# Second copies of the high halves in the first attention's stack: from GpSimd to ScalarE, under an order of its own

## The chip, the cores and the metric

The kernel runs on one core of one Trainium2 chip. The metric is device time in microseconds (us) of one execution. A core has five engines that run side by side, each working through its own queue in order: TensorE (PE in the rows; PEld is its weight load), VectorE (DVE), ScalarE (ACT), GpSimd (POOL) and SyncE (SP, which issues most of the DMA). They wait for one another only through semaphores.

## What is computed

A post-norm transformer block on 16 sequences of 256 rows of 128 features: attention with four key heads shared by sixteen query heads, a layer norm, then a second block (pre-norm attention and a mixture of experts, where each row goes to the one expert with the highest gate), and a last layer norm. The part that the change touches is the first attention's queries and keys:

```
q = (x @ w_q).reshape(B, S, 16, 8);  k = (x @ w_k).reshape(B, S, 4, 8)
q = _apply_rope(_rms_norm(q), cos, sin);  k = _apply_rope(_rms_norm(k), cos, sin)
scores = einsum('bqhd,bkhd->bhqk', q, repeat(k)) / sqrt(8)
scores = tanh(scores / 50) * 50      # then causal mask, softmax, @ v, @ w_o
x = layernorm(x + attention);  x = layernorm(x + block2(x))
```

## The kernel before

One sequence of 256 rows is a batch; there are 16 (`n` = 0 to 15), and each lies on 128 partitions as two tiles. Every batch goes through stages named by letters: **a** loads x, projects, rotates and normalises q and k and splits them; **b** computes scores, tanh, exp and mask in six units; **c** multiplies by v, projects and normalises; **d**, **e**, **f** are the second attention and the gate, with eight units in d and e; **g** is the expert part, in 40 tiles of 128 rows, some of it as early as batch 12.

A step, such as `a_stack` of batch 5, is a short function on one engine. The table `ORDER` gives each step of each batch a rank; every engine issues its own steps in the order of their ranks. So the table, written out by hand as numbers, sets all queues. Each engine's queue is in order: a step that waits holds everything behind it on that engine.

The scores' matmuls take float16, so q and k are each split into a high half and a remainder. `a_sum` (VectorE, L1085 to L1093) makes the mean squares; `a_pow` (GpSimd, L1411) takes them to the power -1/2 (for batches 0 and 1 `a_root` does this on VectorE); `a_split` (VectorE) multiplies (L1121, `qn`), casts the high half into columns 0 to 7 of each head's 32 columns of `stack1` (L1126, step name `hi`), and puts the remainder into columns 24 to 31 (L1128, step name `lo`). `a_stack` (GpSimd, helper `move` at L1414) then makes four copies so that one product of 32 columns gives all cross terms. Queries are 128x256 elements, keys 128x64. After it `a_qT` (TensorE, L725, eight transposes) and `a_kT` (L733) turn the stack, VectorE copies the result (`qs`, L1134, and `kT`, L1139), and the scores' matmuls of `b_sc` (L749) start. `d_stack` uses the same helper line L1414 for the second attention: two copies per batch.

Around these, in the same queues: on ScalarE `b_tanh` (L973), `b_exp` (L977), `e_exp` (L1004), and copies out of PSUM such as `a_xTc` (L968), `c_sum` (L982), `f_sum` (L1009), `f_oTc` (L1013), `d_xTc` (L992); on GpSimd `b_mask` (L1430), `c_pow` (L1435), `c_x1` (L1445, L1449), `f_scatter` (L1478); on VectorE `d_max` (L1230).

PSUM is used in turns. `ring_s` has two buffers, used alternately by the units of `b_sc`, `d_mx` and `e_sc` in the order of their ranks; `ring_p` has two for most other products. Before a unit writes, TensorE waits (`claim`) until the reader of the unit two turns back is done: for `b_sc4` that reader is `b_tanh4`.

`w_fill` (L701, or L698 in the shape of four column groups) is a matmul of a blank tile into the buffer that is free next. It computes nothing; 428 of them stand between other TensorE steps.

Of the kernel before, what the change touches and what calls it, by code (L numbers as in the profile page):

```python
# [106 lines left out]
def wait_turn(eng, sem, n, buffers, each):  # L107
# [16 lines left out]
    "a_load": (0, 3, 5, 6, 15, 246, 410, 500, 593, 824, 927, 1050, 1226, 1468, 1509, 1684),  # L124
    "a_xTc": (1, 13, 19, 113, 189, 293, 424, 584, 703, 864, 1002, 1187, 1346, 1511, 1634, 1815),
    "a_xT": (2, 7, 17, 70, 165, 257, 392, 534, 693, 865, 987, 1153, 1292, 1497, 1620, 1785),
    "a_qkv": (4, 12, 64, 128, 224, 377, 506, 652, 822, 984, 1093, 1265, 1422, 1593, 1776, 1898),
    "a_rope": (8, 18, 69, 134, 234, 387, 511, 657, 820, 986, 1114, 1270, 1440, 1607, 1791, 1920),
    "a_sum": (9, 20, 81, 139, 245, 389, 513, 665, 842, 1003, 1143, 1272, 1477, 1617, 1805, 1924),
# [1391 lines left out]
```

## Time and profile before

| | |
|---|---|
| median of three runs | 705.04 us (702.55 to 707.58) |
| the profiled execution | 702.71 us, its span 701.0 us |
| mean granted TensorE clock, share of full | 0.927 |
| PE busy | 570.1 us, 81% |
| DVE busy | 480.9 us, 69% |
| ACT busy | 425.4 us, 61% |
| POOL busy | 416.7 us, 59% |

The span runs from the first to the last instruction; 1.7 us of the profiled execution's own time lie outside it. In rows of groups, the first part says which line, engine and operation, `out<-in` and how many; behind the first bar are the busy time and the mean of one; behind the second the engine's idle time before them and what ended it. In rows of a timeline the first number is the start, the second the duration in us.

### The profile page before, as it was taken

How to read it: one execution, taken by the hardware profiler on the slowest of the kernel's cores; microseconds unless marked ns; L12 is line 12 of the kernel's file. 1: busy time of each engine (PE TensorE's matmuls, PEld its weight loads, DVE VectorE, ACT ScalarE, POOL GpSimd, SP SyncE). 2: the span in 40 equal slices, each digit the busy share in tenths (PEclk: the TensorE clock that was granted, in tenths of full speed). 3: DMA queues.
4: the chain of work that ended last, by engine and by line, in shares of the span. 5: the costliest groups of instructions: out<-in, count | busy, mean ns of one | idle time of the engine just before them, and what ended most of it. 6: DMA issues, size and time to landing. Idle time of an engine off the chain costs nothing.

```text
span 701.0 us, 16358 instructions
## 1 busy us (share of the span) xinstructions
PE 570.1 (81%) x5771; PEld 339.1 (48%) x5771; DVE 480.9 (69%) x1356; ACT 425.4 (61%) x650; POOL 416.7 (59%) x443
## 2 busy tenths in 40 slices
PE   2648888888888878888897898878997899888992
PEld 1324333344445444455454554545553555557992
DVE  3546757868678868587867768687777787635452
ACT  1675376676785666757677596756675654534661
POOL 2469573648486953775757585769544235525664
PEclk9969779899999988799999999899998999999996
DMA  6420000000000100000012301001002022186650
GB/s 146 135 69 2 8 1 9 2 24 1 9 2 25 40 2 6 5 16 10 17 41 62 85 9 36 1 20 60 25 29 62 12 69 91 39 257 183 187 149 6
DMA packets 30143, 34.30 MB, mean 49 GB/s; under 512 B 6970, under 2 KB 21984, under 8 KB 30064
## 3 DMA queue, kind: packets, MB, share of 16 engines
q1 hardware_dynamic: 26096, 25.53, 12.9%
q0 software_dynamic: 2816, 6.43, 2.6%
q10 hardware_dynamic: 1152, 1.30, 0.6%
q8 instruction: 47, 0.77, 0.5%
q14 instruction: 32, 0.26, 0.1%
HBM read 22.37 MB, written 11.27 MB: 48 GB/s over the span
## 4 chain that ended last, share of the span: by engine, by line
PE 40%; DVE 23%; POOL 16%; issue 10%; ACT 7%; SPq 2%; DMA 1%; POOLq 0%; ACTq 0%; DVEq 0%
DVE mx L1230 10%; PE out L877 6%; POOL rs L1411 5%; PE ring_s L863 3%; POOL stack L1414 3%; PE out L762 3%; PE ring_p L943 3%; PE ring_p L701 3%; PE ring_s L843 3%; POOL p L1430 2%; ACT p L1004 2%; PE ring_p L814 2%; ACT p L973 2%; PE ring_s L749 2%; PE ring_p L931 1%
## 5 line engine op out<-in xcount | busy, mean ns | idle before, releaser
L1230 DVE TENSOR_REDUCE mx<-ring_s 128x4 f32<-128x1024 f32 x128 | 152.8, 1218 | 26.9 <-PE ring_s L843 26.1
L1004 ACT ACTIVATE p<-ring_s 128x1024 f32<-128x1024 f32 x128 | 126.3, 1027 | 38.8 <-PE ring_s L863 38.3
L973 ACT ACTIVATE p<-ring_s 128x1024 f32<-128x1024 f32 x96 | 97.1, 1022 | 38.5 <-PE ring_s L749 38.1
L1411 POOL TENSOR_TENSOR rs<-ms,small 128x40 f32<-128x40 f32 x14 | 94.8, 6772 | 27.6 <-DVE ms L1093 27.3
L1414 POOL TENSOR_SCALAR stack<-stack 128x256 f16<-128x256 f16 (+1 forms) x96 | 65.0, 700 | 75.7 <-DVE stack L1222 42.8
L1430 POOL TENSOR_SCALAR_AFFINE_SELECT p<-p 128x512 f32<-128x512 f32 (+1 forms) x96 | 75.8, 798 | 56.4 <-ACT p L977 56.3
L977 ACT ACTIVATE p<-p 128x1024 f32<-128x1024 f32 x96 | 100.2, 1057 | 0.7
L701 PE MATMUL ring_p<-blank 128*128 128x256 f16 x362 | 80.6, 286 | 5.1 <-ACT t_midT L1037 1.9
L877 PE MATMUL out<-p,v 128*32 128x256 f32 x1024 | 69.8, 400 | 1.3 <-DVE rb L1288 1.2
L843 PE MATMUL ring_s<-kc,qs 32*128 32x256 f16 x512 | 51.2, 281 | 20.2 <-DVE mx L1230 13.0
L863 PE MATMUL ring_s<-qs,kc 32*128 32x256 f16 x512 | 49.4, 290 | 10.1 <-DMA qs<-mT 4.5
L1489 POOL DMA_INDIRECT out<-t_y,t_idx x40 | 41.3, 1034 | 16.4 <-DVE t_y L1380 9.0
L701 PEld LDWEIGHTS ring_p<-blank 128*128 128x128 f16 x362 | 32.6, 103 | 37.9 <-issue 25.3
L762 PE MATMUL out<-p,v 128*32 128x256 f32 x512 | 47.0, 443 | 4.5 <-POOL p L1430 4.1
L749 PE MATMUL ring_s<-qs,kT 32*128 32x512 f16 x192 | 40.0, 422 | 9.7 <-DVE mx L1230 4.5
L1484 POOL TENSOR_TENSOR t_rs<-t_ve,small 128x1 f32<-128x1 f32 x40 | 23.5, 591 | 35.8 <-DVE t_idx L1375 35.5
L943 PE MATMUL ring_p<-w_down,t_midT 128*128 x320 | 44.0, 283 | 0.0
L1478 POOL DMA_INDIRECT routed_rows<-row,pos x32 | 32.9, 1027 | 15.4 <-issue 8.1
L877 PEld LDWEIGHTS out<-p,v 128*32 128x32 f32 x1024 | 29.1, 112 | 26.1 <-issue 11.9
L943 PEld LDWEIGHTS ring_p<-w_down,t_midT 128*128 128x128 f32 x320 | 40.5, 199 | 0.0
L843 PEld LDWEIGHTS ring_s<-kc,qs 32*128 32x128 f16 x512 | 15.3, 94 | 51.7 <-DVE mx L1230 26.4
L1037 ACT ACTIVATE t_midT<-ring_p,b_up 128x128 f32<-128x128 f32 x92 | 26.3, 368 | 21.7 <-PE ring_p L931 20.1
(162 smaller groups left out, 1111.5 us busy)
## 6 DMA issues: line engine op xcount, KB each, us to landing
w_up<-in_L_ffn_w SPq DMA_DIRECT2D x40, 256.0 KB, 2.8
t_row<-routed_rows SPq DMA_DIRECT2D x40, 132.0 KB, 2.4
routed_rows<-padrow SPq DMA_DIRECT2D x8, 396.0 KB, 3.2
...
qs<-mT SPq DMA_DIRECT2D x64, 2.0 KB
out<-t_y,t_idx POOLq DMA_INDIRECT x40, 2.4
...
```

The source lines that it names most:

```text
L701: nc.tensor.matmul(spare[:, 0:256], blank[:, 0:P], blank[:, 0:256], start=True, stop=True)
L843: mm = nc.tensor.matmul(bank(f"d_mx{j}", n)[:, z * 512 + g * S:z * 512 + (g + 1) * S], qs2[32 * i:32 * i + 32, n % 2, 2 * k + g, t * P:(t ...
L863: mm = nc.tensor.matmul(bank(f"e_sc{u}", n)[:, j * 512 + v * S:j * 512 + (v + 1) * S], kc2[32 * i:32 * i + 32, n % 2, g, keys * P:(keys + ...
L877: mm = nc.tensor.matmul(out2[32 * c:32 * c + 32, half * S:(half + 1) * S], v2[:, n % 2, keys, 8 * half + 2 * c + v, :], p2[:, u, at:at + S ...
L943: mm = nc.tensor.matmul(bank("g_down", s)[:, 0:D], t_midT[:, s % 2, c * P:(c + 1) * P], w_down[:, bass.ds(e * FF + c * P, D)], start=False ...
L973: nc.scalar.activation(p1[:, u], bank(f"b_sc{u}", n)[:], ACT.Tanh, scale=float(ISQ / CAP)).then_inc(b_s.sem, 1)
L977: nc.scalar.activation(p1[:, u], p1[:, u], ACT.Exp, scale=CAP).then_inc(b_x.sem, 1)
L1004: nc.scalar.activation(p2[:, u], bank(f"e_sc{u}", n)[:], ACT.Exp, scale=float(ISQ)).then_inc(e_s.sem, 1)
L1230: nc.vector.tensor_reduce(mx2[:, t, 2 * pair:2 * pair + 2, 2 * k:2 * k + 2], bank(f"d_mx{j}", n)[:].rearrange("p (z g s) -> p z g s", z=2, ...
L1411: nc.gpsimd.tensor_tensor(rs1[:], ms1[:], half, ALU.pow).then_inc(a_p.sem, 1)
L1414: return nc.gpsimd.tensor_scalar(dst, src, 1.0, None, ALU.mult)
L1430: nc.gpsimd.affine_select(out=w, in_=w, compare_op=ALU.is_ge, fill=0.0, base=0, pattern=[[0, w.shape[1]], [1, P]], channel_multiplier=-1). ...
```

## The change

Two of the four copies of `a_stack` move to a new ScalarE step `a_hi`: those that copy the high half (queries to columns 8 to 15, keys to columns 16 to 23). They need only `hi`, which VectorE finishes one instruction before `lo`. GpSimd keeps the two copies of the remainder. `a_qT` waits for both.

```diff
+        a_h = steps("a_h", "copy")
...
             def a_qT(n):
                 pe.wait_ge(a_p.sem, a_p.upto(n, "stack"))
+                pe.wait_ge(a_h.sem, a_h.upto(n, "copy"))
...
+            def a_hi(n):
+                act.wait_ge(a_v.sem, a_v.upto(n, "hi"))
+                s4 = stack1[:].rearrange("p (t h) e -> p t h e", t=T)
+                nc.scalar.copy(s4[:, :, 0:NH, HD:2 * HD], s4[:, :, 0:NH, 0:HD])
+                nc.scalar.copy(s4[:, :, NH:, 2 * HD:3 * HD], s4[:, :, NH:, 0:HD]).then_inc(a_h.sem, 1)
...
             def a_stack(n):
                 pool.wait_ge(a_v.sem, a_v.upto(n, "lo"))
                 s4 = stack1[:].rearrange("p (t h) e -> p t h e", t=T)
-                move(s4[:, :, 0:NH, HD:2 * HD], s4[:, :, 0:NH, 0:HD])
                 move(s4[:, :, 0:NH, 2 * HD:3 * HD], s4[:, :, 0:NH, 3 * HD:])
-                move(s4[:, :, NH:, HD:2 * HD], s4[:, :, NH:, 3 * HD:])
-                move(s4[:, :, NH:, 2 * HD:3 * HD], s4[:, :, NH:, 0:HD]).then_inc(a_p.sem, 1)
+                move(s4[:, :, NH:, HD:2 * HD], s4[:, :, NH:, 3 * HD:]).then_inc(a_p.sem, 1)
```

The whole table `ORDER` is new as well, a line of it before and after:

```diff
-    "a_stack": (14, 39, 111, 187, 283, 433, 555, 714, 908, 1045, 1195, 1365, 1552, 1677, 1851, 1982),
+    "a_hi": (18, 41, 118, 205, 284, 436, 590, 748, 899, 1092, 1232, 1393, 1555, 1692, 1846, 2002),
+    "a_stack": (23, 34, 133, 193, 287, 428, 593, 759, 928, 1083, 1213, 1389, 1546, 1709, 1849, 1993),
```

It keeps the plan in the large (which batches overlap which) and swaps neighbours in every queue; it has 447 `w_fill` instead of 428. Line numbers of the changed kernel are 3 to 10 higher.

ScalarE's queue around the split of batch 8, before. L977 is `b_exp` 2 and 3, L973 `b_tanh` 3 and 4 of batch 7, L1009 `f_sum` of batch 4, L1013 `f_oTc`.

```order
L977 ACTIVATE p<-p 128x1024
L973 ACTIVATE p<-ring_s 128x1024 x2
L1009 COPY sums<-out 128x512
L977 ACTIVATE p<-p 128x1024
L1013 COPY oT<-out 128x256
```

The same place after, where L983 is `b_tanh`, L1019 `f_sum`, L977 and L978 the new `a_hi` of batch 8, L972 `a_xTc`, L1023 `f_oTc`.

```order
L1019 COPY sums<-out 128x512
L983 ACTIVATE p<-ring_s 128x1024
L977 COPY stack<-stack 128x2x16x8
L978 COPY stack<-stack 128x2x4x8
L983 ACTIVATE p<-ring_s 128x1024
L972 COPY xT<-ring_p 128x256
L983 ACTIVATE p<-ring_s 128x1024
L1023 COPY oT<-out 128x256
```

`a_hi` of batch 8 now stands between `b_tanh` 3 and `b_tanh` 4 of batch 7, `f_sum` ahead of both, and `b_exp` 3 has moved past `f_oTc`.

TensorE's queue up to `a_qT` of batch 8 (L725), before. L775 is `f_ob` of batch 4, L749 `b_sc` 5 of batch 7, L843 `d_mx` 6 of batch 5, L781 `f_oT`, L701 fillers.

```order
L775 MATMUL out<-ident,sums 128x128 x4
L749 MATMUL ring_s<-qs,kT 128x512 x2
L701 MATMUL ring_p<-blank 128x256
L843 MATMUL ring_s<-kc,qs 128x256 x4
L781 MATMUL out<-ident,o 128x128 x2
L725 MATMUL ring_p<-identh,stack 128x128 x8
```

The same place after (L779 is `f_ob`, L847 `d_mx`, L753 `b_sc`, L785 `f_oT`, L729 `a_qT`, L704 fillers).

```order
L779 MATMUL out<-ident,sums 128x128 x4
L847 MATMUL ring_s<-kc,qs 128x256 x4
L753 MATMUL ring_s<-qs,kT 128x512 x2
L704 MATMUL ring_p<-blank 128x256
L847 MATMUL ring_s<-kc,qs 128x256 x4
L704 MATMUL ring_p<-blank 128x256 x2
L785 MATMUL out<-ident,o 128x128 x2
L704 MATMUL ring_p<-blank 128x256
L729 MATMUL ring_p<-identh,stack 128x128 x8
```

`d_mx` 5 has moved behind `f_ob`, and three more fillers stand ahead of `a_qT`; `b_sc` 5, which waits for `b_tanh` 4, stands ahead of `a_qT` in both.

GpSimd's queue from `a_pow` of batch 2 (L1411) to that of batch 3, before. L1414 x2 with 2x16x8 and 2x4x8 is `a_stack` of batch 2, L1414 with 32x8 `d_stack` of batch 0, L1445 and L1449 `c_x1` of batch 0, L1430 the masks of batch 1.

```order
L1435 TENSOR_TENSOR rl<-ve,small 128x4
L1430 AFFINE_SELECT p<-p 128x1024
L1414 TENSOR_SCALAR stack<-stack 128x2x16x8 x2
L1414 TENSOR_SCALAR stack<-stack 128x2x4x8 x2
L1430 AFFINE_SELECT p<-p 128x4x128 x2
L1430 AFFINE_SELECT p<-p 128x1024
L1445 TENSOR_SCALAR x<-r,mv,rl 128x128 x2
L1449 TENSOR_TENSOR x1b<-x,b_out 128x256
L1414 TENSOR_SCALAR stack<-stack 128x32x8 x2
```

The same place after (L1424 is the helper `move`, L1438 the masks, L1453 and L1457 `c_x1`).

```order
L1443 TENSOR_TENSOR rl<-ve,small 128x4
L1438 AFFINE_SELECT p<-p 128x1024
L1438 AFFINE_SELECT p<-p 128x4x128 x2
L1453 TENSOR_SCALAR x<-r,mv,rl 128x128 x2
L1457 TENSOR_TENSOR x1b<-x,b_out 128x256
L1424 TENSOR_SCALAR stack<-stack 128x2x16x8
L1424 TENSOR_SCALAR stack<-stack 128x2x4x8
L1438 AFFINE_SELECT p<-p 128x1024
L1424 TENSOR_SCALAR stack<-stack 128x32x8 x2
```

`a_stack` of batch 2 has lost two copies and stands behind two masks and `c_x1`.

## Rows read from the trace of the kernel before

**Rows 1.** The page: busy time, share of the span, instructions; the chain by engine.

```profile
PE 570.1 (81%) x5771; PEld 339.1 (48%) x5771; DVE 480.9 (69%) x1356; ACT 425.4 (61%) x650; POOL 416.7 (59%) x443
...
PE 40%; DVE 23%; POOL 16%; issue 10%; ACT 7%; SPq 2%; DMA 1%; POOLq 0%; ACTq 0%; DVEq 0%
```

**Rows 2.** Chain that ended last, in time: start, us, what (pieces of it).

```profile
19.11 2.67 POOL stack L1414 x4
...
53.14 2.33 POOL stack L1414 x4
55.47 2.21 POOL p L1430 x3
57.69 1.86 POOL x L1445 x2
60.38 1.66 POOL stack L1414 x2
...
243.92 2.40 POOL stack L1414 x4
...
285.87 2.33 POOL stack L1414 x4
...
388.05 2.42 POOL stack L1414 x4
...
416.73 2.33 POOL stack L1414 x4
...
453.07 2.38 POOL stack L1414 x4
455.58 1.09 POOL routed_rows L1478
```

**Rows 3.** GpSimd's groups of instructions, shapes apart.

```profile
L1414 POOL TENSOR_SCALAR stack<-stack 128x256 f16<-128x256 f16 x64 | 53.9, 856 | 75.7 <-DVE stack L1222 42.8 <-DVE stack L1128 32.9
...
L1414 POOL TENSOR_SCALAR stack<-stack 128x64 f16<-128x64 f16 x32 | 11.6, 387 | 0.0
```

**Rows 4.** ScalarE's groups, shapes apart.

```profile
L977 ACT ACTIVATE p<-p 128x1024 f32<-128x1024 f32 x96 | 100.2, 1057 | 0.7
...
L982 ACT COPY sums<-out 128x512 f32<-128x512 f32 x16 | 9.4, 586 | 27.8 <-PE out L767 27.8
...
L968 ACT COPY xT<-ring_p 128x256 f32<-128x256 f32 x16 | 6.0, 373 | 11.9 <-PE ring_p L707 11.9
```

**Rows 5.** Timeline around `a_stack` of batch 8, all engines (start, us).

```profile
240.61 1.02 ACT L973 ACTIVATE p<-ring_s 128x1024 f32<-128x1024 f32 x1 [0.91 <-PE ring_s L749]
...
241.49 1.09 POOL L1430 TENSOR_SCALAR_AFFINE_SELECT p<-p 128x1024 f32<-128x1024 f32 x1
...
241.55 1.38 DVE L1121 TENSOR_TENSOR qn<-rot,rs 128x320 f32<-128x320 f32 x1
...
242.97 0.33 DVE L1126 CAST stack<-qn 128x320 f16<-128x320 f32 x1
...
243.33 0.49 DVE L1128 TENSOR_TENSOR stack<-qn,stack 128x320 f16<-128x320 f32 x1
...
244.66 0.39 PE L749 MATMUL ring_s<-qs,kT 32*128 32x512 f16 x2
...
245.74 0.44 PE L781 MATMUL out<-ident,o 128*128 128x128 f32 x2
...
246.37 0.62 PE L725 MATMUL ring_p<-identh,stack 128*128 128x128 f16 x8 [0.19 <-POOL stack L1414]
```

**Rows 6.** Timeline of VectorE, batch 2's split and batch 0's second stack.

```profile
52.20 0.33 DVE L1126 CAST stack<-qn 128x320 f16<-128x320 f32 x1
...
59.38 0.41 DVE L1222 TENSOR_TENSOR stack<-qk,stack 128x256 f16<-128x256 f32 x1
```

**Rows 7.** Timeline of ScalarE before batch 2's stack.

```profile
45.43 2.95 ACT L977 ACTIVATE p<-p 128x1024 f32<-128x1024 f32 x3
52.61 0.56 ACT L992 ACTIVATE hnT<-ring_p,ln_cols 128x256 f32<-128x256 f32 x1 [4.22 <-PE ring_p L808]
```

**Rows 8.** Timelines around batch 14's stack, ScalarE's and all engines'.

```profile
450.23 1.95 ACT L1004 ACTIVATE p<-ring_s 128x1024 f32<-128x1024 f32 x2
...
452.13 0.33 DVE L1126 CAST stack<-qn 128x320 f16<-128x320 f32 x1
...
454.74 2.80 PE L877 MATMUL out<-p,v 128*32 128x256 f32 x48
```

**Rows 9.** One line's instructions: duration ns min/median/max.

```profile
L1121 DVE TENSOR_TENSOR qn<-rot,rs x16: 478/491/1384, 17.6 to 479.0; 128x320 f32<-128x320 f32 x16
```

**Rows 10.** The page: costliest lines of the chain; the filler's group.

```profile
DVE mx L1230 10%; PE out L877 6%; POOL rs L1411 5%; PE ring_s L863 3%; POOL stack L1414 3%; PE out L762 3%; PE ring_p L943 3%; PE ring_p L701 3%; PE ring_s L843 3%; POOL p L1430 2%; ACT p L1004 2%; PE ring_p L814 2%; ACT p L973 2%; PE ring_s L749 2%; PE ring_p L931 1%
...
L701 PE MATMUL ring_p<-blank 128*128 128x256 f16 x362 | 80.6, 286 | 5.1 <-ACT t_midT L1037 1.9
```

More of the change, by code:

```diff
@@ L123 @@
 ORDER = {
[L124 to L129, printed above, removed]
@@ new lines @@
+    "b_mask5": (78, 140, 224, 366, 518, 673, 782, 980, 1102, 1256, 1442, 1558, 1717, 1869, 2110, 2263),
+    "c_pv3": (79, 130, 229, 378, 524, 680, 819, 988, 1137, 1281, 1456, 1579, 1740, 1904, 2142, 2278),
+    "c_ob": (85, 137, 231, 388, 548, 689, 833, 1005, 1151, 1301, 1484, 1586, 1746, 1931, 2152, 2300),
+    "c_oT": (93, 156, 241, 434, 571, 713, 846, 1038, 1189, 1350, 1490, 1634, 1757, 1948, 2166, 2323),
+    "c_oTc": (95, 158, 242, 444, 588, 734, 844, 1034, 1176, 1339, 1476, 1673, 1754, 1983, 2165, 2326),
@@ new lines @@
+    "a_pow": (96, 143, 259, 400, 561, 729, 863, 1012, 1161, 1325, 1514, 1642, 1816, 1942),
+    "c_r": (98, 175, 239, 460, 600, 749, 884, 1046, 1214, 1366, 1517, 1677, 1777, 2020, 2203, 2348),
+    "c_pow": (100, 161, 243, 467, 630, 780, 912, 1075, 1236, 1382, 1516, 1724, 1776, 1999, 2199, 2324),
+    "c_mo": (101, 177, 247, 476, 619, 772, 890, 1073, 1233, 1380, 1529, 1687, 1782, 2032, 2228, 2354),
+    "c_y": (103, 162, 244, 453, 606, 760, 874, 1041, 1210, 1361, 1519, 1676, 1775, 1985, 2184, 2332),
@@ new lines @@
+    "d_xT": (105, 201, 270, 492, 632, 799, 938, 1088, 1244, 1388, 1568, 1745, 1820, 2038, 2251, 2367),
+    "c_xh": (110, 188, 263, 501, 621, 796, 926, 1081, 1239, 1392, 1575, 1738, 1815, 2046, 2253, 2368),
+    "d_qkv0": (112, 210, 323, 500, 653, 807, 957, 1098, 1255, 1404, 1590, 1758, 1879, 2074, 2258, 2373),
+    "d_xTc": (119, 200, 285, 494, 645, 802, 945, 1097, 1240, 1398, 1576, 1743, 1813, 2034, 2244, 2365),
[4 rows of a table added]
+    "d_hi": (135, 227, 348, 525, 671, 821, 983, 1115, 1264, 1434, 1610, 1773, 1906, 2086, 2269, 2402),
@@ new lines @@
+    "d_lo": (138, 232, 349, 531, 672, 822, 991, 1128, 1277, 1439, 1613, 1805, 1928, 2105, 2270, 2403),
+    "d_stack": (141, 236, 338, 527, 686, 811, 1011, 1130, 1280, 1453, 1628, 1814, 1937, 2100, 2265, 2393),
+    "d_qTc": (148, 253, 375, 552, 711, 855, 996, 1136, 1296, 1492, 1658, 1839, 1954, 2111, 2298, 2434),
+    "d_qT": (151, 245, 353, 538, 703, 836, 992, 1140, 1290, 1487, 1644, 1826, 1943, 2115, 2287, 2439),
+    "d_kT": (152, 252, 374, 546, 708, 842, 1004, 1149, 1293, 1489, 1646, 1830, 1951, 2155, 2295, 2443),
@@ new lines @@
+    "p_bT": (164,),
+    "p_bTc": (165,),
+    "d_mx0": (166, 281, 406, 559, 710, 858, 1017, 1160, 1310, 1505, 1664, 1836, 1961, 2192, 2301, 2446),
+    "d_kTc": (171, 254, 379, 557, 712, 860, 1006, 1147, 1295, 1496, 1661, 1848, 1956, 2159, 2307, 2437),
[15 rows of a table added]
+    "d_m": (222, 377, 470, 676, 864, 937, 1059, 1187, 1451, 1540, 1808, 2022, 2047, 2212, 2398, 2519),
+    "d_nm": (225, 336, 454, 617, 794, 943, 1076, 1211, 1375, 1561, 1760, 1933, 2081, 2264, 2366, 2495),
+    "d_mT": (235, 341, 469, 622, 789, 949, 1067, 1227, 1371, 1564, 1778, 1965, 2099, 2254, 2360, 2502),
@@ new lines @@
+    "d_mTc": (240, 343, 472, 624, 792, 951, 1063, 1225, 1370, 1563, 1761, 1986, 2087, 2245, 2358, 2511),
[20 rows of a table added]
+    "f_sum": (299, 464, 605, 739, 893, 1053, 1169, 1340, 1477, 1691, 1898, 2076, 2205, 2353, 2452, 2587),
+    "f_ob": (310, 465, 618, 746, 915, 1051, 1181, 1362, 1506, 1689, 1930, 2077, 2220, 2362, 2483, 2581),
+    "f_o": (319, 498, 636, 742, 922, 1068, 1191, 1368, 1510, 1694, 1953, 2091, 2217, 2377, 2482, 2582),
+    "f_oT": (327, 489, 629, 770, 930, 1065, 1215, 1369, 1552, 1734, 1949, 2116, 2232, 2369, 2487, 2588),
@@ new lines @@
+    "f_rank": (404, 553, 706, 849, 976, 1154, 1294, 1446, 1625, 1852, 2039, 2164, 2321, 2427, 2530, 2620),
+    "f_place": (408, 567, 701, 862, 994, 1163, 1303, 1447, 1647, 1862, 2051, 2167, 2327, 2421, 2532, 2627),
+    "f_res": (429, 562, 718, 852, 1008, 1212, 1355, 1407, 1640, 1845, 2024, 2170, 2328, 2391, 2506, 2603),
+    "f_scatter": (439, 768, 771, 854, 1146, 1267, 1448, 1452, 1853, 1997, 2045, 2194, 2390, 2442, 2517, 2623),
+    "p_plan": (1457, 2171, 2535, 2638),
+    "g_row": (1480, 1495, 1557, 1582, 1597, 1631, 1654, 1810, 2005, 2163, 2210, 2225, 2349, 2374, 2383, 2417, 2420,
+        2559, 2560, 2563, 2611, 2617, 2628, 2647, 2648, 2659, 2668, 2693, 2700, 2705, 2723, 2734, 2742, 2747, 2760,
+        2787, 2792, 2806, 2811, 2831),
@@ new lines @@
+    "g_w": (1486, 1504, 1573, 1617, 1649, 1653, 1751, 1982, 1987, 2092, 2201, 2309, 2345, 2347, 2387, 2392, 2406,
+        2544, 2551, 2579, 2616, 2630, 2632, 2634, 2644, 2649, 2675, 2699, 2717, 2741, 2745, 2750, 2757, 2764, 2772,
+        2789, 2804, 2824, 2840, 2845),
+    "g_hTc": (1494, 1498, 1648, 1668, 1732, 1874, 1950, 1992, 2147, 2237, 2334, 2361, 2395, 2428, 2492, 2499, 2518,
+        2574, 2595, 2614, 2622, 2650, 2656, 2664, 2676, 2688, 2694, 2709, 2712, 2731, 2754, 2762, 2765, 2776, 2790,
+        2805, 2823, 2839, 2842, 2869),
@@ new lines @@
+    "g_hT": (1509, 1533, 1641, 1672, 1727, 1854, 1946, 1973, 2138, 2223, 2319, 2363, 2410, 2418, 2480, 2490, 2512,
+        2575, 2584, 2607, 2626, 2640, 2667, 2673, 2683, 2689, 2702, 2715, 2732, 2738, 2752, 2756, 2774, 2777, 2791,
+        2799, 2818, 2829, 2844, 2861),
+    "g_mid": (1537, 1538, 1696, 1841, 1919, 1991, 2003, 2103, 2202, 2306, 2341, 2371, 2429, 2470, 2503, 2534, 2553,
+        2598, 2605, 2641, 2651, 2655, 2665, 2679, 2695, 2706, 2710, 2729, 2753, 2759, 2763, 2783, 2786, 2808, 2819,
+        2826, 2841, 2852, 2863, 2870),
@@ new lines @@
+    "g_up": (1539, 1549, 1674, 1835, 1922, 1969, 1979, 2101, 2157, 2303, 2356, 2381, 2425, 2475, 2493, 2520, 2538,
+        2578, 2599, 2633, 2642, 2657, 2678, 2684, 2697, 2708, 2716, 2736, 2739, 2748, 2768, 2780, 2793, 2796, 2802,
+        2817, 2828, 2849, 2853, 2867),
+    "g_rs": (1616, 1723, 1847, 1880, 2018, 2123, 2139, 2187, 2262, 2415, 2424, 2455, 2477, 2505, 2570, 2585, 2593,
+        2613, 2635, 2652, 2660, 2670, 2680, 2681, 2703, 2727, 2737, 2758, 2771, 2779, 2800, 2813, 2822, 2830, 2832,
+        2836, 2858, 2860, 2865, 2874),
@@ new lines @@
+    "g_down": (1620, 1629, 1786, 1851, 1976, 2085, 2117, 2133, 2218, 2320, 2416, 2460, 2466, 2514, 2552, 2565, 2567,
+        2618, 2637, 2643, 2663, 2682, 2692, 2704, 2713, 2725, 2743, 2746, 2755, 2770, 2788, 2798, 2807, 2820, 2837,
+        2838, 2851, 2854, 2868, 2876),
+    "g_z": (1639, 1650, 1803, 1865, 2000, 2108, 2118, 2131, 2256, 2376, 2414, 2458, 2461, 2513, 2550, 2561, 2580,
+        2615, 2639, 2653, 2658, 2690, 2698, 2701, 2719, 2722, 2730, 2744, 2766, 2775, 2782, 2785, 2803, 2812, 2834,
+        2835, 2848, 2855, 2866, 2873),
@@ new lines @@
+    "g_out": (1651, 1936, 1962, 2021, 2089, 2197, 2336, 2397, 2423, 2454, 2469, 2481, 2540, 2572, 2597, 2624, 2625,
+        2629, 2646, 2662, 2677, 2687, 2696, 2735, 2740, 2761, 2767, 2773, 2784, 2794, 2821, 2825, 2827, 2833, 2850,
+        2857, 2862, 2864, 2871, 2877),
+    "g_y": (1659, 1765, 1872, 1934, 2049, 2109, 2158, 2196, 2271, 2422, 2448, 2489, 2509, 2558, 2562, 2571, 2586,
+        2636, 2654, 2685, 2686, 2691, 2711, 2718, 2728, 2733, 2749, 2769, 2778, 2781, 2797, 2801, 2810, 2814, 2846,
+        2847, 2856, 2859, 2872, 2875),
@@ L308 @@
+    "q_sp": (2568,),
 }
@@ L1040, in g_mid @@
                 last.then_inc(relu_s.sem, 1)
-            parts = dict(a_xTc=a_xTc, c_sum=c_sum, c_oTc=c_oTc, d_xTc=d_xTc, d_mTc=d_mTc, f_sum=f_sum, f_oTc=f_oTc,
+            parts = dict(a_xTc=a_xTc, a_hi=a_hi, c_sum=c_sum, c_oTc=c_oTc, d_xTc=d_xTc, d_mTc=d_mTc, f_sum=f_sum, f_oTc=f_oTc,
                          f_hTc=f_hTc, p_bTc=p_bTc, g_hTc=g_hTc, g_mid=g_mid)
```

119 lines of the change are left out of this document (29 added, 90 removed), and 171 rows, old and new, of the table ORDER.

## The prediction, made before the changed kernel ran

> **What bounds the kernel now.** I read the busy shares first: TensorE is busy 81% of the span, VectorE 69%, ScalarE 61%, GpSimd 59% [rows 1]. No engine is full, so a second look is needed: the chain of waits that ended last. It runs 40% over TensorE, 23% over VectorE, 16% over GpSimd and only 7% over ScalarE [rows 1]. So a microsecond of GpSimd's work has a far better chance to be on the path than one of ScalarE's: 16% of 701 is 112 us out of 416.7 busy, against 49 out of 425.4. Then I looked for `a_stack` in that chain in order of time. Four moves at a time are `a_stack`, two are `d_stack`. `a_stack` stands there for 7 of the 16 batches: 0, 2, 8, 9, 12, 13 and 14 [rows 2]. In batches 8 and 0 TensorE starts the transposes right behind it (243.92 + 2.40 = 246.32, transposes at 246.37, [rows 2, 5]); in batches 2 and 14 the chain goes on in GpSimd's own queue, with masks and with the scatter [rows 2].
>
> **What is removed.** Per batch one move of 256 and one of 64 elements leave GpSimd, of means 856 and 387 ns, half of `a_stack` [rows 3]. The four take 2.33 to 2.42 us in the chain and 2.67 in batch 0 [rows 2], so half is 1.17, and 1.33 in batch 0. Over 16 batches GpSimd loses some 19 us of its 416.7. On the path:
>
> - Batch 0: 1.33 us, since nothing else stands between the remainder's cast and the transposes.
> - Batches 8, 9, 12, 13, 14: 5 x 1.17 = 5.9 us.
> - Batch 2: the new order puts two masks and `c_x1` ahead of `a_stack`. The path there is GpSimd's queue up to `d_stack` of batch 0 at 60.38 [rows 2]. What that waits for, VectorE's last cast, ends at 59.38 + 0.41 = 59.8 [rows 6], so the stall that is next in line leaves at most 0.6; I take 0.5.
>
> Gross gain: 7.7 us.
>
> **What is added on ScalarE.** No row of before shows a float16 copy in runs of eight elements on this engine. The nearest rows: a copy of 512 elements takes 586 ns, one of 256 takes 373 [rows 4], so 0.83 ns an element and 160 ns besides; 64 elements then take about 213, the pair 586. Neighbours overlap: three exps take 2.95 us instead of 3 x 1.057 [rows 4, 7], 0.11 less at each join. Lower bound 0.48, which I take as 0.5. Upper bound, if short runs cost ScalarE what they cost GpSimd: 856 + 387 = 1.24 us. I choose the low one because per element the nearest rows are of the same engine. 16 pairs are 8.0 us. What is on the path of that: ScalarE's chain share is 49 of 425.4, 0.115 of each us, so 0.9 us (2.3 at the upper bound). The pair itself delays the transposes nowhere that I found in the chain: it starts with `hi`, some 0.5 us before GpSimd can start with `lo` (243.33 + 0.49 against 242.97 + 0.33 in batch 8, [rows 5]) and takes 0.5 against 1.17.
>
> **The wait that is added.** This is the part that speaks against the change. ScalarE's queue now stops at `a_hi` until VectorE has cast `hi`. I looked at what stood there before.
>
> - Batch 2: ScalarE sat idle 4.22 us up to 52.61, and `hi` ends at 52.53 [rows 6, 7]; only the pair's own 0.5 us is pushed into `d_xTc`.
> - Batch 8: `b_tanh` 4 of batch 7 ran at 240.61, and `hi` ends at 243.30 [rows 5]. Behind `a_hi` it starts at 243.30 + 0.1 + 0.5 = 243.9, 3.3 us later, and ends at 244.9. `b_sc` 5 needs its buffer and is queued on TensorE ahead of the transposes; it ran at 244.66 before. Now: 244.9, then 0.39 for it, 0.39 for `d_mx` 6, four fillers at 0.286 [rows 10], 0.44 for `f_oT` [rows 5]: the transposes start near 247.2 instead of 246.37. So batch 8 does not bring its 1.17 and costs 0.8 besides: 2.0 off.
> - Batch 14: two second-attention exps ran from 450.23, and `hi` ends at 452.46 [rows 8]. Behind `a_hi` they start at 453.1, 2.8 us later; with another short step between them the last ends near 455.6, and the matmuls by v that ran from 454.74 [rows 8] are pushed by about 1.0. I take 1.0 off.
>
> Net of the waits: 7.7 - 2.0 - 1.0 = 4.7 us.
>
> **The fillers.** 19 more, at 286 ns in the filler's group, are 5.4 us of TensorE. The filler's line has 3% of the chain, 21 us of 80.6 busy [rows 10], so 0.26 of each: 1.4 us, between nothing (each in a gap) and 5.4. They could also lift the granted clock, 0.927 of full now. At full clock throughout, TensorE's 40% of the chain would shrink by up to 7%, some 20 us; but before has 428 of them and stands at 0.927, so I take nothing for 19 more.
>
> **VectorE beside GpSimd.** The product `qn` takes 491 ns in the median and 1384 at most [rows 9]; the long one at 241.55 lies beside a mask of GpSimd that runs from 241.49 to 242.58 and ends just ahead of the cast [rows 5]. So GpSimd's work can hold VectorE's, here by 0.9 us. 32 fewer GpSimd instructions give fewer such holds. Bounds: nothing, and the 19 us that they last; I take 1.0, the size of one such hold, because only the batches whose `qn` is at its median are shown to be free of it. The Trainium skill, in "GPSIMD Engine Reference", section "Specifications", says that GpSimd's way to SBUF is shared with VectorE and contended when VectorE has two SBUF inputs; by that rule, the trace agrees in the one row, and moving the copies to ScalarE could be worth more than the moves' own time; without it the sum would be 1.0 us smaller.
>
> **The sum.** 4.7 + 1.0 - 0.9 - 1.4 = 3.4 us. The rows come from an execution of 702.71 us, span 701.0; it would be 699.3. Against the median of the runs, 705.04, it is 701.6 us.
>
> **The rivals.**
>
> GpSimd's relief counts in every batch (0.28). GpSimd loses 16 x 1.17 + 0.16 = 18.9 us, and the new order is built for the shorter step, so a stretch where `a_stack` is off the chain today may be packed tighter. Then 18.9 - 0.9 - 1.4 = 16.6 and the time is 688.4; partial success reaches up to 697. For it: GpSimd waited for `lo` ahead of `a_stack` for 32.9 us in total [rows 3], so the copies start as soon as their data is there and end a serial leg. Against it: only 7 batches are on the chain, and TensorE is at 81%.
>
> ScalarE's queue is the loser (0.22). The place is `a_hi`, waiting for `hi` with tanh and exp behind it. If all its time counts: 8.0 for the pairs, 3.3 and 2.8 for the waits in batches 8 and 14, 14.1 in all. With the fillers' 1.4 and the gross gain of 7.7: 7.8 us slower, 712.8. It makes the kernel slower than before once ScalarE's part on the path is over 6.3 us (7.7 - 1.4), and slower by over 1% from 13.4 us on. Against it: ScalarE is 7% of the chain.
>
> Nothing to be seen (0.08). The copies leave the chain but TensorE or VectorE, next in line, take its place everywhere, and the swaps of neighbours cancel: 705.
>
> **How the numbers follow.** The forecast of 701.6 has 0.42, with a range of its own from 697 to 706. The range of 8 in 10 goes from 690 to 713: it takes in most of the first rival and all but half of the second. A difference of 1% (7 us) is about what a measurement of this kernel can tell from none. Faster by over 1%, below 698: the first rival's 0.28 and 0.08 of the forecast, 0.36. Slower by over 1%, above 712: 0.13 of the second rival and 0.02 of the forecast's tail, 0.15. Within: 0.32, 0.09 and 0.08, 0.49.
>
> **What would show it.** In the profile after, GpSimd's moves should be 64 instead of 96, with 8 to 10 us more on ScalarE and 19 less on GpSimd; the pair should take near 0.5 us, and over 1 us would prove the price wrong. `a_stack` should last 1.2 us, and in batch 0 the transposes should start 1.3 us earlier. ScalarE should show idle time in front of the new copies, released by VectorE's cast, 2 to 3 us long in batches 8 and 14; if it is missing, or above 10 us in total, the wait was priced wrong. The chain should have 2% rather than 3% in the moves. If its GpSimd share falls and TensorE's or VectorE's rises by as much, the last rival holds.

## The result: slower by 1.9%

| | before | changed |
|---|---|---|
| median | 703.79 us (701.01 to 707.58) | 716.88 us (715.2 to 721.84) |
| the profiled execution's span | 701.0 us | 713.5 us |
| mean granted TensorE clock | 0.927 | 0.912 |

The ratio is 1.0194, with 95% between 1.0122 and 1.0266. 701.6 was forecast, with a range of 690 to 713, so the time lies outside the range. In every ratio here, executions that something outside the kernel slowed down are left out. The medians below are of all executions, 4 to 12 for most kernels, so a ratio is not always the quotient of two medians.

The page of the changed kernel: busy time of each engine, the granted clock in tenths in 40 slices of the span, and the chain that ended last by engine.

```profile
PE 587.8 (82%) x5811; PEld 343.5 (48%) x5811; DVE 484.0 (68%) x1356; ACT 431.7 (61%) x682; POOL 400.9 (56%) x411
...
PEclk9967789799999999989998799998998899999997
...
PE 42%; DVE 22%; issue 13%; POOL 10%; ACT 8%; DMA 2%; SPq 2%; POOLq 0%; ACTq 0%; DVEq 0%
```

GpSimd lost 15.8 us of work and ScalarE gained 6.3 (416.7 and 425.4 before, [rows 1]), where 19 and 8 to 10 were forecast; GpSimd's moves alone lost the 19 (65.5 and 46.7 us in the groups), and its other work took 3 us longer. In the chain, `issue` is time for which the profile shows no wait. GpSimd's share of the chain fell from 16% to 10%. That is what the change is meant to do, and still the span is 12.5 us longer. TensorE's busy time rose by 17.7 us, of which the 19 fillers more account for 5.4 at the forecast's 286 ns.

GpSimd's groups, shapes apart: the moves, now 48 and 16 instead of 64 and 32 [rows 3].

```profile
L1424 POOL TENSOR_SCALAR stack<-stack 128x256 f16<-128x256 f16 x48 | 40.8, 860 | 65.6 <-DVE stack L1232 33.3 <-DVE stack L1138 32.2
...
L1424 POOL TENSOR_SCALAR stack<-stack 128x64 f16<-128x64 f16 x16 | 5.9, 367 | 0.0
```

ScalarE's groups: the new copies.

```profile
L977 ACT COPY stack<-stack 128x256 f16<-128x256 f16 x16 | 6.5, 407 | 13.8 <-DVE stack L1136 13.8
...
L978 ACT COPY stack<-stack 128x64 f16<-128x64 f16 x16 | 4.0, 248 | 0.0
```

They take 407 and 248 ns, and ScalarE sat idle 13.8 us before them until VectorE had cast the high half; the group counts five such waits.

Where is the loss? The profiled executions are cut into stretches in which about the same steps lie. As neighbours are swapped, a border is good to 1 or 2 us. The columns are start and end, length, busy time of PE, PEld, DVE, ACT and POOL with instructions, granted clock, DMA share, GB/s. Before:

```profile
0.00:100.00 100.00, 62.34 (x480) 30.49 (x484) 54.47 (x152) 49.13 (x61) 60.17 (x63) 0.85 0.23 63
100.00:240.00 140.00, 119.97 (x1336) 62.88 (x1327) 105.80 (x253) 96.45 (x120) 89.00 (x89) 0.94 0.04 14
240.00:340.00 100.00, 83.72 (x907) 44.94 (x907) 76.22 (x183) 64.86 (x79) 62.82 (x60) 0.91 0.02 7
340.00:420.00 80.00, 69.29 (x797) 39.89 (x785) 58.40 (x169) 58.24 (x83) 53.97 (x57) 0.98 0.17 47
420.00:560.00 140.00, 120.08 (x1250) 70.55 (x1249) 107.20 (x285) 89.02 (x132) 80.80 (x90) 0.94 0.10 31
560.00:701.00 141.00, 114.66 (x1027) 90.35 (x1026) 78.83 (x318) 67.66 (x177) 69.90 (x87) 0.94 0.41 122
```

Changed:

```profile
0.00:100.00 100.00, 61.89 (x507) 30.80 (x507) 55.11 (x152) 50.77 (x68) 55.12 (x55) 0.84 0.24 65
100.00:240.00 140.00, 123.14 (x1318) 62.53 (x1318) 104.65 (x253) 97.66 (x126) 84.84 (x80) 0.92 0.04 12
240.00:342.00 102.00, 85.45 (x927) 43.85 (x915) 77.23 (x183) 67.50 (x87) 60.56 (x57) 0.95 0.04 11
342.00:431.00 89.00, 77.77 (x777) 44.16 (x773) 61.47 (x171) 60.09 (x89) 54.52 (x54) 0.88 0.15 43
431.00:574.00 143.00, 127.12 (x1294) 72.83 (x1296) 107.54 (x285) 87.59 (x134) 73.40 (x78) 0.92 0.13 37
574.00:713.50 139.50, 112.44 (x1007) 89.30 (x1006) 78.03 (x316) 68.08 (x178) 72.49 (x90) 0.94 0.39 114
```

In this trace about 9 of the 12.5 us lie in one stretch, 80 us long before and 89 after. There the granted clock is 0.88 instead of 0.98, and TensorE is busy 77.8 us for fewer recorded products than before had in 69.3. That looks like the seat of the loss. It is not a fixed one, as the same kernel on another chip shows further down.

### The profile page after: what moved, and what is told of

Read it like the earlier page. It is cut to its first block, busy times and chain, and to the rows that moved or that the text cites. A ratio compares the mean times of both kernels' runs of the same rounds, so it can differ in the third digit from the quotient of the medians.

```text
span 713.5 us, 16454 instructions
## 1 busy us (share of the span) xinstructions
PE 587.8 (82%) x5811; PEld 343.5 (48%) x5811; DVE 484.0 (68%) x1356; ACT 431.7 (61%) x682; POOL 400.9 (56%) x411
## 4 chain that ended last, share of the span: by engine, by line
PE 42%; DVE 22%; issue 13%; POOL 10%; ACT 8%; DMA 2%; SPq 2%; POOLq 0%; ACTq 0%; DVEq 0%
DVE mx L1240 7%; PE out L881 7%; POOL rs L1421 4%; PE out L766 4%; PE ring_p L704 3%; PE ring_s L847 3%; PE ring_s L867 3%; PE ring_p L818 2%; PE ring_p L935 2%; PE ring_p L947 2%; ACT p L983 2%; PE ring_s L753 2%; POOL out L1497 2%; ACT p L1014 2%; ACT p L987 2%
## 5 line engine op out<-in xcount | busy, mean ns | idle before, releaser
L983 ACT ACTIVATE p<-ring_s 128x1024 f32<-128x1024 f32 x96 | 97.0, 1023 | 44.4 <-PE ring_s L753 44.1
L1438 POOL TENSOR_SCALAR_AFFINE_SELECT p<-p 128x512 f32<-128x512 f32 (+1 forms) x96 | 75.6, 798 | 71.0 <-ACT p L987 70.9
L704 PE MATMUL ring_p<-blank 128*128 128x256 f16 x374 | 85.0, 289 | 6.1 <-DVE qs L1144 2.2
L1424 POOL TENSOR_SCALAR stack<-stack 128x256 f16<-128x256 f16 x64 | 46.2, 737 | 65.6 <-DVE stack L1232 33.3
L881 PE MATMUL out<-p,v 128*32 128x256 f32 x1024 | 73.3, 408 | 1.1 <-DVE rb L1298 1.0
L847 PE MATMUL ring_s<-kc,qs 32*128 32x256 f16 x512 | 53.2, 294 | 15.5 <-DVE mx L1240 8.9
L704 PEld LDWEIGHTS ring_p<-blank 128*128 128x128 f16 x374 | 33.8, 103 | 40.7 <-issue 25.4
L766 PE MATMUL out<-p,v 128*32 128x256 f32 x512 | 50.0, 470 | 3.2 <-POOL p L1438 3.0
L753 PE MATMUL ring_s<-qs,kT 32*128 32x512 f16 x192 | 40.4, 427 | 14.6 <-DVE mx L1240 6.1
L847 PEld LDWEIGHTS ring_s<-kc,qs 32*128 32x128 f16 x512 | 15.3, 95 | 49.5 <-DVE mx L1240 21.0
```

The source lines that it names most:

```text
L704: nc.tensor.matmul(spare[:, 0:256], blank[:, 0:P], blank[:, 0:256], start=True, stop=True)
L766: nc.tensor.matmul(out1[32 * c:32 * c + 32, half * S:(half + 1) * S], v1[:, n % 2, 0, i, v, :], p1[:, 3 * half + g, j * 512 + v * S:j * 51 ...
L847: mm = nc.tensor.matmul(bank(f"d_mx{j}", n)[:, z * 512 + g * S:z * 512 + (g + 1) * S], qs2[32 * i:32 * i + 32, n % 2, 2 * k + g, t * P:(t ...
L881: mm = nc.tensor.matmul(out2[32 * c:32 * c + 32, half * S:(half + 1) * S], v2[:, n % 2, keys, 8 * half + 2 * c + v, :], p2[:, u, at:at + S ...
L983: nc.scalar.activation(p1[:, u], bank(f"b_sc{u}", n)[:], ACT.Tanh, scale=float(ISQ / CAP)).then_inc(b_s.sem, 1)
L1438: nc.gpsimd.affine_select(out=w, in_=w, compare_op=ALU.is_ge, fill=0.0, base=0, pattern=[[0, w.shape[1]], [1, P]], channel_multiplier=-1). ...
```

## The experiments

All but e2 carry the new code (the ScalarE copies). What varies is the table `ORDER`. On three chips the kernel before took 704 us; on two others it took 723, with a lower mean clock (0.914 over its executions there, against 0.925 and 0.927 on two of the first three). Ratios are always against the kernel before on the same chip.

**Code and table apart.** e1 has the new code with the old table; `a_hi` is put in where before's trace shows the cast ending. e2 is the old code with the new table.

```diff
 # e1, against before
+    "a_hi": (14, 36, 110, 184, 275, 430, 560, 738, 914, 1067, 1198, 1391, 1552, 1692, 1853, 1985),
-    "a_stack": (14, 39, 111, 187, ...
+    "a_stack": (15, 41, 114, 191, ...
```

> The new code (two copies on ScalarE) under the table of the kernel before, with its 428 fillers; a_hi of each batch is put into ScalarE's queue behind the step that ran there when the trace of before shows VectorE's cast of the high half ending, so that ScalarE waits little. Theory A (the new table costs the time, the move itself does not): 699 to 704, at or a little below the kernel before. Theory B (ScalarE's new copies and waits cost it): 712 to 718, as the changed kernel.

> The old code (four copies on GpSimd) under the new table, a_hi left out, its 447 fillers kept. Theory A: 715 to 725, as slow as the changed kernel or slower by up to the 1.17 us a batch that GpSimd keeps. Theory B: 702 to 707, as the kernel before.

| | old table | new table |
|---|---|---|
| old code | 704.37 | 718.64, ratio 1.0208 (1.0147 to 1.0269) |
| new code | 703.02, ratio 0.9982 (0.9954 to 1.001) | 716.88, ratio 1.0194 (1.0122 to 1.0266) |

The whole loss comes with the table, with either code. With either table the copies themselves move the time by less than the intervals. And ScalarE's waiting in itself is not the cause: with the old table it waits almost as long in total and nothing is lost. ScalarE's group in e1:

```profile
L979 ACT COPY stack<-stack 128x256 f16<-128x256 f16 x16 | 6.5, 406 | 12.6 <-DVE stack L1138 12.6
```

e1's page, busy time and chain:

```profile
PE 570.1 (81%) x5771; PEld 341.0 (49%) x5771; DVE 478.7 (68%) x1356; ACT 432.6 (62%) x682; POOL 397.3 (57%) x411
...
PE 42%; DVE 23%; issue 11%; ACT 10%; POOL 9%; SPq 2%; DMA 2%; POOLq 0%; ACTq 0%; DVEq 0%
```

GpSimd's share fell here too, from 16% to 9%, and the time stayed. Its place was taken by TensorE (42% for 40%), ScalarE (10% for 7%) and issue (11% for 10%). Compared step by step with before, e1 is 3.6 us ahead from 80 to 220 us, and only 0.7 to 1.1 from 500 us on. In that trace the relief exists early and is given back. In e14, the same kernel on another chip, the lead is 1 to 2 us up to 220 us, at most 2.8 (from 280 to 300 us), and 0.7 us or less from 360 us on. So how much was gained early varies from one execution to the next, and that almost nothing is left does not.

**Steps and fillers apart.** The table holds two things: the order of the steps and the places of the fillers. e5 has the new order of steps with the old fillers, e6 the old order with the new ones (so many ahead of each TensorE step as the other table has there, but 27 and 28 of them a little later), e7 and e8 have none.

```diff
 # e7 and e8: the line is gone;  e5: 428 entries, e6: 447, placed as said
-    "w_fill": (3, 6, 30, 49, 50, ...
```

> The new code and the new table's steps, but with the 428 fillers of the old table, each ahead of the TensorE step that it stood ahead of there (27 of them moved later so that no filler waits for a buffer that cannot come free yet). If the extra low-clock time of the changed kernel comes from where its fillers stand: 703 to 708 and a granted clock near 0.925. If it comes from the order of the steps: 712 to 720, clock near 0.91.

> The new code and the old table's steps with ScalarE's copies put in as in the run of new code under the old table, but with the 447 fillers of the new table (28 moved later). If the fillers' places cost the time: 712 to 720, clock near 0.91. If the steps do: 702 to 706, clock near 0.925.

> The new code and the new table's steps without any filler; nothing of the result is left out, since fillers compute nothing. Fillers hold the clock, so it should be well below 0.91 and the time above 716. If the steps' order is at fault, it is 10 us or more slower than the old steps without fillers; if the fillers' places are, the two are within 5 us.

> The new code and the old table's steps (with ScalarE's copies put in) without any filler. The partner of the run before: above 703 by what the clock loses; 10 us or more below the new steps without fillers if the steps' order is at fault, within 5 us if the fillers' places are.

| fillers | old order of steps | new order of steps |
|---|---|---|
| its own | 703.02 (e1) | 716.88 (changed) |
| the other table's | 720.52, 1.0285 (1.02 to 1.0371) | 731.93, 1.0402 (1.0317 to 1.0487) |
| none: ratio | 1.0194 (1.0077 to 1.031) | 1.0245 (1.0146 to 1.0344) |
| none: median | 716.19 (e8; 707.0 of the two that are not disturbed) | 719.80 (e7; 716.0 of three) |
| none: span of the profiled execution, clock | 700.6, 0.868 | 712.1, 0.853 |

The runs without fillers scatter (702.73, 711.22, 721.15 and 912.86 for e8; 713.83, 716.02, 723.58 and 726.89 for e7). Their lowest times and their profiled spans stand 11 us apart, the medians of the undisturbed ones 9, but all medians only 4, and the ratios 0.5%, well inside the intervals. So they point at the order of the steps and do not prove it.

The four kernels with fillers have to be read as a square. With the old fillers the new order of steps costs 28.9 us (731.93 - 703.02); with the new ones it is 3.6 faster (716.88 - 720.52). With the old steps the new fillers cost 17.5 us (720.52 - 703.02); with the new steps they save 15.1. The mean effect of the steps is 12.6 us, that of the fillers 1.2, but larger than both is whether the two belong together: in the places of the other table the same kind of filler costs 15 to 18 us, which I had not priced. And 19 more of them can't be the loss, since with the new steps 447 fillers in their own places are faster than 428 in foreign ones.

From the pages of e8, then of e7, the busy times:

```profile
PE 544.3 (78%) x5145; PEld 320.4 (46%) x5145; DVE 478.5 (68%) x1356; ACT 431.1 (62%) x682; POOL 398.3 (57%) x411
```

```profile
PE 561.2 (79%) x5145; PEld 323.9 (45%) x5145; DVE 484.6 (68%) x1356; ACT 432.0 (61%) x682; POOL 400.4 (56%) x411
```

The same 5145 products take TensorE 544.3 us in one order and 561.2 in the other, in these two executions.

**Which part of the table.** e3 has the old table up to `a_qT` of batch 11, which runs near 350 us, and the new one behind; e4 the reverse.

```diff
-    "a_qT": (..., 1387, 1554, 1696, 1870, 1996),
+    "a_qT": (..., 1399, 1556, 1705, 1853, 2006),  # e3
+    "a_qT": (..., 1412, 1577, 1720, 1895, 2022),  # e4
```

> The new code, with the old table for all steps up to a_qT of batch 11 (about 350 us) and the new table for all behind. The two traces of before and after differ by 2 us up to there and by 9 more between 350 and 430 us. Theory A with the loss in that later stretch: 712 to 716. If the loss needs what the new table did earlier, or is ScalarE's in the first eleven batches: 703 to 707.

> The new code, with the new table up to a_qT of batch 11 and the old table behind it. Theory A with the loss behind 350 us: 702 to 706. If it is the first part that costs: 712 or more.

e3: 706.32, ratio 1.0022 (0.9987 to 1.0057). e4: 714.69, ratio 1.0162 (1.0076 to 1.0247). The table behind 350 us, where the trace of the changed kernel shows nearly all of its loss, has little part in causing it: the cause stands in the table ahead of it. e4's own trace bears that out: compared step by step with before, it is 6.4 us behind at 340 us and 9.8 at 380, though its table is the old one there, and it loses nothing more from there on.

I then cut finer: e9 has the new table up to 100 us, e11 up to 246, e12 only from 350 to 420. e10 is e1 with one swap of the new table, in GpSimd's queue: `a_stack` of batch 2 behind two masks and `c_x1`.

```diff
-    "a_stack": (15, 41, 114, 191, ...   # e1
+    "a_stack": (15, 41, 125, 191, ...   # e10, and e18
```

> The new code, the new table up to a_qT of batch 4 (about 104 us), the old table behind. The traces of the changed kernel and of new code under the old table differ by 3.0 us at 80 to 100 us: the old table gains 3.6 there against the kernel before, the new one 0.6. If the loss is made piece by piece where the rows stand: 705 to 707. If the early swaps alone set off the whole loss of the first part: 712 or more. If they do not matter: 702 to 704.

> New code under the old table, one place of the new table: GpSimd's a_stack of batch 2 behind two masks of batch 1 and c_x1 of batch 0. In the changed kernel VectorE's xh, qn and cast take 1.70, 0.93 and 0.46 us beside these, against 1.36, 0.48 and 0.33, and a_stack ends 3.1 us later. If this place makes most of the early loss: 704.5 to 707. If only its own microsecond: 703 to 704.5.

> The new code, the new table up to a_qT of batch 8 (about 246 us), the old table behind. The new table up to 350 us took 714.7, 11.7 above new code under the old table. If the loss is spread evenly over the stages: 709 to 712. If it lies ahead of 100 us: as the run to 100 us. If it lies between 246 and 350 us: 703 to 706.

> The new code, the new table only from behind a_qT of batch 11 up to a_qT of batch 13 (about 350 to 420 us), the old table elsewhere. The trace of the changed kernel loses 9 us more in this stretch, with a granted clock of 0.66 from 380 to 400 us. If the swaps of this stretch are the cause: 709 to 713. If the low clock there came from what went before: 702 to 705.

These four ran on a chip where the kernel before takes 722.67 us (35 executions, 718.44 to 727.51). Ratios: e9 1.0037 (1.0018 to 1.0056), e10 1.0032 (1.0007 to 1.0058), e11 1.0023 (1.0005 to 1.0042), e12 1.005 (1.0021 to 1.0079). All are small, and they cannot be added up to 2%. Neither the changed kernel nor e1 ran on that chip, so it can't be said whether even these 0.2 to 0.5% come from the parts of the table. The next four repeated both ends of the comparison on another chip, with two parts of the table.

> The changed kernel itself, on one chip with the three others of this call. The last four runs were on a chip where the kernel before takes 722.7 us instead of 704.4, and all four part-new tables lay within 0.2 to 0.5% of it. If the new table's loss is a property of the table: ratio to the kernel before 1.015 to 1.022 here too. If it depends on the chip: within 1.005 where the chip is one of the slower ones.

> New code under the old table again: 0.995 to 1.001 of the kernel before on any chip, if the move itself is worth 0 to 3 us. If it was the chip of the first call: 1.002 to 1.005.

> The new table up to 350 us, the old one behind, again: 1.012 to 1.018 of the kernel before if the first part's swaps cost 10 us everywhere; 1.002 to 1.005, as the tables that are new up to 100 or 246 us, if that was the chip.

> The old table up to a_qT of batch 4 (about 104 us), the new one behind: the changed kernel without its first stretch. If the first 100 us are where the table loses: 1.000 to 1.005 of the kernel before. If the loss lies behind, or is spread: 1.012 to 1.020.

Here the kernel before took 704.08.

| new table | median | ratio |
|---|---|---|
| whole (e13) | 717.29 | 1.0201 (1.0163 to 1.0239) |
| nowhere (e14, which is e1) | 703.02 | 0.999 (0.996 to 1.002) |
| up to 350 us (e15, which is e4) | 713.95 | 1.0162 (1.0119 to 1.0205) |
| from 100 us on (e16) | 713.94 (712.68 of the five that the ratio counts) | 1.0126 (1.0077 to 1.0175) |

On such a chip 2.0 - 1.3 = 0.7% belong to the first 100 us, 1.6 - 0.7 = 0.9% to those up to 350, and 0.2 to 0.4% to the rest; each difference is uncertain by 0.6% or more. So no single one of these three parts is shown to carry the loss.

e13 is the changed kernel once more. Its stretches, cut as above:

```profile
240.00:345.00 105.00, 91.30 (x919) 46.02 (x915) 76.36 (x182) 67.42 (x87) 60.07 (x57) 0.87 0.03 11
345.00:430.00 85.00, 71.89 (x798) 41.25 (x794) 62.50 (x173) 60.47 (x90) 56.15 (x55) 0.98 0.15 45
430.00:573.00 143.00, 128.24 (x1282) 74.05 (x1278) 105.52 (x283) 87.68 (x134) 71.84 (x77) 0.88 0.12 37
```

The stretch behind 345 us has a clock of 0.98 here, as before had, and it is 5 us longer than in before instead of 9. The low clock (0.87) and 5 us more are in the stretch ahead of it, where the first execution had 0.95 and was 2 longer. So where the loss shows in one trace varies from one execution to the next, and the sum does not: 713.5 and 713.4 us of span.

**One swap.** e17 is the changed kernel with that one swap undone; e18 repeats e10.

```diff
-    "a_stack": (23, 34, 133, 193, ...   # changed
+    "a_stack": (23, 34, 114, 193, ...   # e17
```

> The changed kernel with one swap undone: GpSimd's a_stack of batch 2 stands ahead of the two masks and c_x1 again. The changed kernel is at 1.020 of the kernel before. If this swap starts the early loss (3 us behind new code under the old table by 80 us): 1.013 to 1.017. If it is one of many small ones: 1.018 to 1.021.

> New code under the old table with that one swap put in, again, since the first time it ran on a chip 18 us slower for all kernels, without new code under the old table beside it. If the swap starts the early loss: 1.003 to 1.008 of the kernel before, against 0.998 to 0.999 without it. If it is worth its own microsecond at most: 0.998 to 1.001.

They ran on a chip where the kernel before takes 723.41 us. e17 is at 1.0011 (0.9981 to 1.004), e18 at 1.0024 (0.9994 to 1.0054). e17 has nearly the whole new table and loses nothing there. Two readings remain: that one swap carries most of the loss, or the new table costs nothing on a chip where the old one is slow as well. The first is unlikely: on the chip at 704 us, e16 leaves the first 100 us as they were, this swap with them, and still loses 1.3%. The changed kernel itself has not run on a chip at 723 us, so neither is shown.

What the swap does in its place can be seen. Timeline of batch 2 in the changed kernel:

```profile
50.44 2.26 POOL L1438 TENSOR_SCALAR_AFFINE_SELECT p<-p 128x1024 f32<-128x1024 f32 x3
50.50 1.70 DVE L1199 TENSOR_SCALAR xh<-r,mv,rl 128x128 f32<-128x128 f32 x2 [1.98 <-POOL rl L1443]
52.12 0.93 DVE L1131 TENSOR_TENSOR qn<-rot,rs 128x320 f32<-128x320 f32 x1
52.71 2.03 POOL L1453 TENSOR_SCALAR x<-r,mv,rl 128x128 f32<-128x128 f32 x2
53.08 0.46 DVE L1136 CAST stack<-qn 128x320 f16<-128x320 f32 x1
53.58 0.41 ACT L977 COPY stack<-stack 128x256 f16<-128x256 f16 x1 [5.05 <-DVE stack L1136]
...
55.52 1.20 POOL L1424 TENSOR_SCALAR stack<-stack 128x256 f16<-128x256 f16 x2
```

And in e1, with the old order:

```profile
49.63 1.09 POOL L1440 TENSOR_SCALAR_AFFINE_SELECT p<-p 128x1024 f32<-128x1024 f32 x1
49.69 1.36 DVE L1201 TENSOR_SCALAR xh<-r,mv,rl 128x128 f32<-128x128 f32 x2 [5.85 <-POOL rl L1445]
50.98 0.48 DVE L1133 TENSOR_TENSOR qn<-rot,rs 128x320 f32<-128x320 f32 x1
51.49 0.33 DVE L1138 CAST stack<-qn 128x320 f16<-128x320 f32 x1
...
52.43 1.19 POOL L1426 TENSOR_SCALAR stack<-stack 128x256 f16<-128x256 f16 x2 [1.72 <-DVE stack L1140]
```

Three things hold `a_stack` back by 3.1 us. GpSimd's queue is already 0.8 us later ahead of these rows (its masks start at 50.44 instead of 49.63). VectorE's pair `xh`, its product and its cast take 3.09 us instead of 2.17 while GpSimd's masks and `c_x1` run beside them. The remaining 1.4 us `a_stack` stands in line behind 2.03 us of `c_x1` and its sum.

The product L1131 starts beside GpSimd's masks and ends 0.35 us after the last of them (52.12 + 0.93 against 50.44 + 2.26). The long product of batch 8 in the kernel before ends 0.35 us after its mask as well (241.55 + 1.38 against 241.49 + 1.09, [rows 5]), and so do, within 0.01 us, the other six products over 0.6 us in the traces of before and changed. Each starts beside a mask or GpSimd's sum `row<-x,r` and is held until that has ended, with no semaphore between them. Beside `c_x1` and `c_pow` the product takes its usual 0.48 us in the same traces.

The Trainium skill, "GPSIMD Engine Reference", section "Specifications", states contention between these two engines over SBUF, for VectorE instructions with two SBUF inputs or in a 2-port mode, and that section gives no size. By that rule, the trace agrees in the product, which has two inputs and is 0.45 us longer. The other two are longer as well, by 0.34 and 0.13 us; whether they run in a 2-port mode, no run shows.

## Why the prediction was wrong, point by point

**The step that failed: the table was priced as neutral.** The prediction took three places from the new order (batches 2, 8 and 14) and 1.4 us for the fillers, and for the rest went by "keeps the plan in the large". The table costs 718.64 - 704.37 = 14.3 us with the old code and 717.29 - 703.02 = 14.3 with the new, where the largest term of the working was 7.7. The working had no row for it. In its last rival, too, "the swaps of neighbours cancel", and no rival let them cost time. That the swaps cancel is what failed. With every queue permuted, the places that were looked up in the chain of before need not be the places that decide; which ones do, the runs don't show.

**The gross gain of 7.7 us** was too large as well. Its form held in single places. The pair takes about 0.56 us (0.5 forecast), and GpSimd's part 1.21 us (1.17). In batch 0 the transposes start 1.1 us earlier than before (1.3 forecast):

```profile
19.40 0.41 ACT L977 COPY stack<-stack 128x256 f16<-128x256 f16 x1
19.45 1.21 POOL L1424 TENSOR_SCALAR stack<-stack 128x256 f16<-128x256 f16 x2 [13.95 <-DVE stack L1138]
...
20.71 1.03 PE L729 MATMUL ring_p<-identh,stack 128*128 128x128 f16 x8 [1.61 <-POOL stack L1424]
```

But with the old table, where nothing else is changed, the copies are worth 1.1 to 1.4 us (703.02 against 704.08 and 704.37), and no gain at all lies inside both intervals. With the prediction's own port and ScalarE terms, 7.7 + 1.0 - 0.9, the sum for e1 would be 7.8. Seven places on GpSimd in the chain are not seven independent gains. The chain of e1 suggests why: GpSimd's share fell by 7 points and TensorE's, ScalarE's and issue's rose by 6, so other work stood close behind. That is the mechanism of the last rival, which had 0.08; the copies by themselves did what it said.

**VectorE beside GpSimd** was put at 1.0 us of gain. The hold is real, as the rows of batch 2 show. But moving the copies did not lessen it: over their 485 ns each, the 16 products take 1.8 us more in all in before, 1.7 in the changed kernel, and 0.9 and 2.0 in e1 and e14. It depends on which instructions happen to meet.

**ScalarE's hold** was forecast at 3.0 us for batches 8 and 14. The mechanism is there: ScalarE waits 2.17 and 2.90 us in front of these two pairs, 2 to 3 were forecast. In the changed kernel, batch 8:

```profile
244.09 0.33 DVE L1136 CAST stack<-qn 128x320 f16<-128x320 f32 x1
...
244.45 0.41 ACT L977 COPY stack<-stack 128x256 f16<-128x256 f16 x1 [2.17 <-DVE stack L1136]
...
244.91 1.01 ACT L983 ACTIVATE p<-ring_s 128x1024 f32<-128x1024 f32 x1
...
245.98 0.39 PE L753 MATMUL ring_s<-qs,kT 32*128 32x512 f16 x2 [0.24 <-ACT p L983]
```

The pair, then `b_tanh` 4, then the scores' product that waits for it, as described; the transposes followed at 248.16, 1.8 us later than before and 1.0 later than forecast; VectorE's cast itself came 1.1 us later than before. All idle time before the pairs is 13.8 us, above the 10 that I had named as the mark of a wrong price. Yet e1 waits 12.6 us in the same way and is not slower, and e2, which has no such wait, is as slow as the changed kernel. So it costs nothing that can be measured. The second rival's number, 712.8, came near by luck: its mechanism acts and is not what costs.

**The fillers** were put at 1.4 us for the 19 more. Their number is not what counts: moving them to the places of the other table costs 15 to 18 us, in either direction of the exchange.

**The clock** was left out "for 19 more fillers". The changed kernel has 0.912 and 0.905, before has 0.927, and e1 and e14 have 0.925 and 0.926. The traces know two levels, full and half. So a mean of 0.927 over 701.0 us is 2 x (1 - 0.927) x 701.0 = 102 us at half clock; e1 has 105, the changed kernel 126 and 136. Without fillers it is 185 us in the old order and 209 in the new. In each pair the new order spends over 20 us more at half clock, with fillers or without.

What such time costs can be read in one kernel. Among executions of the kernel before, the span grows by 3.5 us for each 0.01 of mean clock lost on one chip and by 4.1 on another (17 executions each), which is 0.25 to 0.3 us for each us at half clock. The two traces of the changed kernel say 0.2: with 17 or 18 us more at half clock, a stretch is 3 or 4 us longer. By the slope, 0.019 less (the means over all executions on the chip of e13 are 0.927 before and 0.908 changed) would go with 7 to 8 of the 13 us, and leave the rest to another cause. That is a correlation. Across kernels the slope does not hold: e8 has 0.868, 0.057 less than e1, and its profiled span is 700.6 us. Whether the new order lowers the clock and so costs time, or leaves gaps and so lowers the clock, no run here separates.

**What stays open**: which swaps in the new order do the harm. On the chips at 704 us it lies for the most part in the first 350 us of the table, and the finer cuts (e9 to e12, e17) only ran on chips at 723 us, where none of them was more than 0.5% slower. Whether the loss is absent there, and why, stays open too. So does what makes those chips slower; the kernel before has a lower clock on them.
